# First loads of a routed low-rank kernel split into partition halves over two queues, chunk 0 taken base weights first, seven warm-up products

## The reference

```
base   = x @ W.T                                   # 2048 x 512
logits = x @ Wr.T + 5.0 * one_hot(id of sequence)  # 2048 x 8
topw, topi = top_k(logits, 2); weights = softmax(topw)
gates  = weights at topi, 0 elsewhere              # 2048 x 8
h      = x @ A.T                                   # 2048 x 8 x 16
out    = x + base + 2.0 * sum over experts (h * gates) @ B
```

## Time and profile before

| | |
|---|---|
| median of 3 runs | 80.04 us (79.7, 80.2, 80.04) |
| the profiled execution's own time | 79.61 us |
| its span, first to last instruction | 77.8 us |
| TensorE busy | 74.0 us (95%) |
| VectorE, ScalarE, GpSimd busy | 48.9, 22.4, 22.6 us |

### The profile page before, as it was taken

One profiled execution on the slowest core, in us unless ns is written; L12 is line 12 of the kernel. 1 busy time (PEld: TensorE's weight loads), 2 busy tenths in 40 slices (PEclk: granted clock), 3 DMA queues, 4 the chain that ended last, 5 costly groups with the idle time before them and its releaser, 6 DMA issues.

```text
span 77.8 us, 1631 instructions
## 1 busy us (share of the span) xinstructions
PE 74.0 (95%) x505; PEld 70.3 (90%) x505; DVE 48.9 (63%) x220; ACT 22.4 (29%) x57; POOL 22.6 (29%) x26
## 2 busy tenths in 40 slices
PE   5979999999999999999999999999999999999960
PEld 2349999899999999999999999999999999999950
DVE  0098958879854829283755739283855739787750
ACT  1647901523503314140504113140404023122100
POOL 4039542055160505123060605123060606000000
PEclk9999999999999999999999999999999999999999
DMA  0999991795597399989900000450000072032143
GB/s 10 308 406 401 419 430 60 167 420 230 83 417 313 54 365 440 383 241 402 388 25 0 0 0 0 177 227 0 0 0 0 0 297 107 0 135 95 44 139 135
DMA packets 3893, 14.24 MB, mean 183 GB/s; under 512 B 432, under 2 KB 1328, under 8 KB 3632
## 3 DMA queue, kind: packets, MB, share of 16 engines
q1 hardware_dynamic: 3600, 13.52, 46.8%
q10 hardware_dynamic: 288, 0.67, 2.2%
HBM read 9.99 MB, written 4.19 MB: 182 GB/s over the span
## 4 chain that ended last, share of the span: by engine, by line
PE 90%; DMA 5%; DVE 1%; ACT 1%; SPq 0%; issue 0%
PE heads_ps L429 43%; PE base_ps L429 28%; PE heads_ps L469 5%; PE base_ps L469 5%; DMA first_sb<-in_first 5%; PE base_ps L473 2%; PE heads_ps L473 2%; PE ghT_ps L460 2%; PE base_ps L453 2%; DVE out_sb L421 1%; ACT w_hi L235 1%; SPq L165 0%; PE warm_ps L460 0%
## 5 line engine op out<-in xcount | busy, mean ns | idle before, releaser
L207 POOL TENSOR_TENSOR x_lo<-xT_sb,x_hi 128x512 fp32r<-128x512 f32 x14 | 18.1, 1294 | 39.0 <-ACT x_hi L242 37.2
L429 PE MATMUL heads_ps<-w_hi,x_hi 128*128 128x392 f32 x64 | 22.2, 357 | 0.0
L429 PE MATMUL heads_ps<-w_hi,x_lo 128*128 128x392 f32 x64 | 21.1, 342 | 0.0
L429 PE MATMUL heads_ps<-w_lo,x_hi 128*128 128x392 f32 x64 | 21.1, 340 | 0.0
L429 PE MATMUL base_ps<-w_hi,x_hi 128*128 128x256 f32 x60 | 16.5, 285 | 0.4 <-ACT w_hi L235 0.4
L429 PE MATMUL base_ps<-w_hi,x_lo 128*128 128x256 f32 x60 | 16.7, 281 | 0.0
L429 PE MATMUL base_ps<-w_lo,x_hi 128*128 128x256 f32 x60 | 16.3, 281 | 0.0
L294 DVE TENSOR_TENSOR ghT_lo<-ghT_ps,ghT_hi 128x128 fp32r<-128x128 f32 x15 | 4.3, 290 | 14.9 <-ACT ghT_hi L246 14.8
L246 ACT ACTIVATE ghT_hi<-ghT_ps 128x128 fp32r<-128x128 f32 x15 | 4.1, 275 | 29.5 <-PE ghT_ps L460 29.5
L429 PEld LDWEIGHTS heads_ps<-w_hi,x_hi 128*128 128x128 f32 x64 | 11.7, 188 | 0.9 <-ACT x_hi L232 0.5
L429 PEld LDWEIGHTS base_ps<-w_hi,x_hi 128*128 128x128 f32 x60 | 11.2, 188 | 0.8 <-ACT w_hi L235 0.8
(11 more groups left out here) (51 smaller groups left out, 98.1 us busy)
## 6 DMA issues: line engine op xcount, KB each, us to landing
x_sb<-in_x SPq DMA_DIRECT2D x4, 768.0 KB, 5.6
out<-out_sb SPq DMA_DIRECT2D x4, 768.0 KB, 4.4
xT_sb<-in_xT SPq DMA_DIRECT2D x3, 768.0 KB, 4.3
xT_sb<-in_xT SPq DMA_DIRECT2D x1, 1024.0 KB, 6.3
x_sb<-in_x SPq DMA_DIRECT2D x1, 1024.0 KB, 9.8
first_sb<-in_first SPq DMA_DIRECT2D x2, 454.0 KB, 5.3
out<-out_sb SPq DMA_DIRECT2D x2, 256.0 KB, 2.0
out<-out_sb SPq DMA_DIRECT2D x4, 128.0 KB, 1.7
```

The lines of the kernel that those rows point to most:

```text
L207: nc.gpsimd.tensor_tensor(x_lo[:, s, :], xT_sb[:, t - len(FIRST), :], x_hi[:, s, :].bitcast(FP32), ALU.subtract).then_inc(x_lo_made, 1)
L429: return nc.tensor.matmul(dst, xs[:, s, chunks[k]], ws[:, k, cols], start=(k == 0 and n == 0), stop=(k == KC - 1 and n == last_n))
```

## The change

The loads of `first` are cut by partitions: SyncE loads partitions 0 to 63 and ScalarE partitions 64 to 127 of every piece, by the same function. The pieces are chunk 0's tokens, ids and base weights as one (516 columns), chunk 0's heads weights (392 columns), and chunks 1, 2 and 3 whole. Both halves count up the same semaphore, so every wait on one is now for 32. The base columns come first in the weight table. VectorE rounds the base weights of chunk 0 (its upper part and remainder first), ScalarE the heads weights of chunk 0. TensorE takes chunk 0's three pairs of base products first, then the heads products. The warm-up is seven products instead of nine.

```diff
@@ -25,7 +25,7 @@
 SLOTS = 3
 LANG_BIAS = 5.0
 SCALING = 2.0
-WARM_UP = 9
+WARM_UP = 7
 WIDTH = HEADS + BASE
 
 
...
@@ -141,13 +140,20 @@
         out_made = sem("out_made")
         last_x_placed = sem("last_x_placed")
 
-        heads_cols, base_cols, all_cols = slice(0, HEADS), slice(HEADS, WIDTH), slice(0, WIDTH)
+        base_cols, heads_cols, all_cols = slice(0, BASE), slice(BASE, WIDTH), slice(0, WIDTH)
         chunks = [slice(k * P, (k + 1) * P) for k in range(KC)]
         first_x = [first_sb[:, k, 0:FIRST_X].rearrange("p (t c) -> p t c", c=P) for k in range(KC)]
         ids_at = FIRST_X
         ids_sb = first_sb[:, 0, ids_at:ids_at + 1].bitcast(I32)
         w_sb = first_sb[:, :, FIRST_X + IDS:]
-        w = first[:, :, FIRST_X + IDS:]
+
+        ahead_of = FIRST_X + IDS + BASE
+
+        def load_half(engine, rows):
+            engine.dma_start(first_sb[rows, 0, 0:ahead_of], first[rows, 0, 0:ahead_of]).then_inc(first_landed, 16)
+            engine.dma_start(first_sb[rows, 0, ahead_of:], first[rows, 0, ahead_of:]).then_inc(second_landed, 16)
+            for k in range(1, KC):
+                engine.dma_start(first_sb[rows, k, :], first[rows, k, :]).then_inc(chunk_landed[k - 1], 16)
 
         block = ctx.enter_context(nc.Block())
 
@@ -162,10 +168,7 @@
             def load_xT(t, n, landed):
                 load(xT_sb, xT, t - len(FIRST), n, landed)
 
-            sp.dma_start(first_sb[:, 0, 0:FIRST_X + IDS], first[:, 0, 0:FIRST_X + IDS]).then_inc(x_landed, 16)
-            sp.dma_start(w_sb[:, 0, base_cols], w[:, 0, base_cols]).then_inc(wb_landed, 16)
-            for k in range(2, KC):
-                sp.dma_start(first_sb[:, k, :], first[:, k, :]).then_inc(chunk_landed[k - 1], 16)
+            load_half(sp, slice(0, P // 2))
             load_xT(2, 1, xT_third)
             sp.dma_start(b_sb[:, :], b).then_inc(b_landed, 16)
 
@@ -250,14 +253,13 @@
                 nc.scalar.activation(e2[:, :], top[:, 0:1], ACT.Exp, scale=-1.0,
                                      bias=top[:, 1:2]).then_inc(e2_made, 1)
 
-            act.dma_start(w_sb[:, 0, heads_cols], w[:, 0, heads_cols]).then_inc(wh_landed, 16)
-            act.dma_start(first_sb[:, 1, :], first[:, 1, :]).then_inc(chunk_landed[0], 16)
-            act.wait_ge(x_landed, 16)
+            load_half(act, slice(P // 2, P))
+            act.wait_ge(first_landed, 32)
             chunk_upper(0)
-            act.wait_ge(wb_landed, 16)
-            w_upper(0, base_cols)
+            act.wait_ge(second_landed, 32)
+            w_upper(0, heads_cols)
             for k in range(1, KC):
-                act.wait_ge(chunk_landed[k - 1], 16)
+                act.wait_ge(chunk_landed[k - 1], 32)
                 chunk_upper(k)
                 w_upper(k, base_cols if k == 1 else all_cols)
             x_upper(2, 2, xT_third, 16)
@@ -358,22 +360,22 @@
                 nc.vector.tensor_tensor(w_lo[:, k, cols], w_sb[:, k, cols], w_hi[:, k, cols].bitcast(FP32),
                                         ALU.subtract).then_inc(w_lo_made, 1)
 
-            def heads_upper(k):
-                nc.vector.tensor_copy(w_hi[:, k, heads_cols], w_sb[:, k, heads_cols]).then_inc(wh_hi_made, 1)
-
-            dve.wait_ge(wh_landed, 16)
-            heads_upper(0)
-            dve.wait_ge(wh_hi_made, 1)
-            w_lower(0, heads_cols)
-            dve.wait_ge(w_hi_made, 1)
+            def w_upper(k, cols):
+                nc.vector.tensor_copy(w_hi[:, k, cols], w_sb[:, k, cols]).then_inc(first_hi_made, 1)
+
+            dve.wait_ge(first_landed, 32)
+            w_upper(0, base_cols)
+            dve.wait_ge(first_hi_made, 1)
             w_lower(0, base_cols)
             dve.wait_ge(expert_made, 1)
-            dve.wait_ge(x_landed, 16)
+            dve.wait_ge(first_landed, 32)
             nc.vector.tensor_scalar(bias[:, :], expert[:, :], ids_sb, LANG_BIAS, ALU.is_equal,
                                     ALU.mult).then_inc(bias_made, 1)
-            dve.wait_ge(chunk_landed[0], 16)
-            heads_upper(1)
-            dve.wait_ge(wh_hi_made, 2)
+            dve.wait_ge(w_hi_made, 1)
+            w_lower(0, heads_cols)
+            dve.wait_ge(chunk_landed[0], 32)
+            w_upper(1, heads_cols)
+            dve.wait_ge(first_hi_made, 2)
             w_lower(1, heads_cols)
             dve.wait_ge(w_hi_made, 2)
             w_lower(1, base_cols)
@@ -503,26 +505,27 @@
 
             warm(WARM_UP)
             pe.wait_ge(chunk_hi_made, 1)
-            pe.wait_ge(wh_hi_made, 1)
+            pe.wait_ge(first_hi_made, 1)
+            for t in FIRST:
+                base_product(t, 0, 0)
+            pe.wait_ge(w_lo_made, 1)
+            for t in FIRST:
+                base_product(t, 0, 1)
+            pe.wait_ge(chunk_lo_made, 1)
+            for t in FIRST:
+                base_product(t, 0, 2)
+            pe.wait_ge(w_hi_made, 1)
             for t in FIRST:
                 heads_product(t, 0, 0)
-            pe.wait_ge(w_hi_made, 1)
-            for t in FIRST:
-                base_product(t, 0, 0)
-            pe.wait_ge(chunk_lo_made, 1)
             for t in FIRST:
                 heads_product(t, 0, 2)
-                base_product(t, 0, 2)
-            pe.wait_ge(w_lo_made, 1)
+            pe.wait_ge(w_lo_made, 2)
             for t in FIRST:
                 heads_product(t, 0, 1)
-            pe.wait_ge(w_lo_made, 2)
-            for t in FIRST:
-                base_product(t, 0, 1)
             for k in range(1, KC):
                 pe.wait_ge(chunk_hi_made, k + 1)
                 if k == 1:
-                    pe.wait_ge(wh_hi_made, 2)
+                    pe.wait_ge(first_hi_made, 2)
                 else:
                     pe.wait_ge(w_hi_made, k + 1)
                 for t in FIRST:
@@ -606,7 +609,7 @@
 
     x, W, Wr, A, B = (np.asarray(a) for a in (x, L0_cond_W, L0_cond_Wr, L0_cond_A, L0_cond_B))
     tokens = x.reshape(P, TILES, KC, P)
-    weights = np.concatenate([W[BASE:], A.reshape(ER, D), Wr, W[:BASE]]).reshape(WIDTH, KC, P).transpose(2, 1, 0)
+    weights = np.concatenate([W[:BASE], W[BASE:], A.reshape(ER, D), Wr]).reshape(WIDTH, KC, P).transpose(2, 1, 0)
     xT = tokens.transpose(3, 1, 2, 0)
     ahead = len(FIRST)
     first_x = xT[:, :ahead].transpose(0, 2, 1, 3).reshape(P, KC, FIRST_X)
```

More of the change, by code:

```diff
@@ L94, in cond_resid_program @@
         warm_ps = ps("warm_ps")
-        x_landed = sem("x_landed")
+        first_landed = sem("first_landed")
         xT_third = sem("xT_third")
@@ L102, in cond_resid_program @@
         x_last = sem("x_last")
-        wh_landed = sem("wh_landed")
-        wb_landed = sem("wb_landed")
+        second_landed = sem("second_landed")
         chunk_landed = [sem(f"chunk_landed{k}") for k in range(1, KC)]
@@ L112, in cond_resid_program @@
         bias_made = sem("bias_made")
-        wh_hi_made = sem("wh_hi_made")
+        first_hi_made = sem("first_hi_made")
         w_hi_made = sem("w_hi_made")
```

## The result

The changed kernel takes 82.97 us (median of six executions, 82.63 to 83.43) against 79.89: a ratio of 1.039, 95% interval 1.035 to 1.043. It is **3.1 us slower**; 80.3 was forecast, with a range up to 81.8. The profiled execution is the slowest of the six, 83.43 with a span of 81.6, 3.8 us more than before. An execution over 1.5% above the fastest of its kernel is left out of a ratio; where there are such executions, all times are given.

What follows compares the result with a forecast made beforehand. TensorE's dense stream was taken as the bound, so the end shifts with chunk 1's start: 7.06 against 6.83, +0.23 us. Added to the median of 80.04 this gave 80.27, say 80.3; range 79.5 to 81.8.

Steps and rivals of the forecast that it cites:

- the price of a 64-row issue on ScalarE's queue: Each of three issues added ahead of ScalarE's table load was put at 0.46 us, with bounds 0.34 and 0.68.
- the landing of the halves: First pieces land by about 3.6, covered by 0.76 us until 4.36; chunk 2 must land by 7.75, before at 6.6.
- worth nothing by itself: Before TensorE's first product: seven warm-up products end 0.4 us earlier than nine, but nothing waits for their end; no gain.
- ScalarE's head: At ScalarE's start: five issues push the table load to 3.06 and the first rounding from 3.57 to 4.36, 0.79 us delay.
- The upper bound, 5.02: Latest first rounding on ScalarE, reckoned with 0.68 us for a 64-row issue, the longest load issue.
- First products: TensorE in chunk 0: first base product at 4.83, 0.23 hole for GpSimd's remainders, chunk 1 at 7.06 against 6.83, +0.23 us.
- the half-rate rival: Transfers of half the partitions move at half rate; chunk 3 starts 3.0 us late, 83.0; decides below 304 GB/s; chance 0.22.
- its 10.03 for chunk 2: Moment chunk 2 lands if halves move at 203 GB/s; before, it was taken up at 6.60.
- The milder price that the prediction gave: Halves moving at 270 GB/s add 0.6 us on top of the forecast sum, giving 80.9.
- The clock rival: TensorE's clock falls in the 0.9 us pause before 4.83, products cost double, 1.45 us lost: 81.7; chance 0.10.
- four signs of being wrong: Table load before 2.5; first rounding waits for transfer; ScalarE awaits chunk 2 beyond 7.75; products over 0.18 and 0.12 apart.

Runs made afterwards that it cites:

- ScalarE's issues: Kernel before with three more 64-byte-a-row transfers into an unread spare tile, issued by ScalarE ahead of its table load: 80.15 us, ratio 1.0043.
- the stage by itself: Kernel before with six stages of differently cut transfers put ahead, each waited for; the change's partition halves moved 265 GB/s, 9.69 us a stage.
- the whole-transfer kernel: Changed kernel, seven warm-up products kept, with whole 128-partition transfers on the two queues instead of halves: 81.34 us, ratio 1.017.

## Why the prediction was wrong, step by step

Three steps failed: the price of a 64-row issue on ScalarE's queue, the landing of the halves, and the warm-up that was "worth nothing by itself". None of them gives the 3.1 us alone. Column halves in place of partition halves took back 1.2 (81.79), ten more warm-up products 0.6 (82.39), column halves and twelve warm-up products together 1.9 (81.07). Some 1.2 is left over the kernel before. ScalarE's issues and the column order cost 0.3 each in their own runs; the rest, late landings most likely, no run separates.

- **ScalarE's head: right in mechanism, mis-sized.** The row taken, 0.46, is that of a 128-row issue. The three added issues took 0.64 each, and the first two, which the sum left at the old price, are 64-row issues as well: the third began at 2.24, not 1.66. That makes 0.54 + 0.58 = 1.12, and the first rounding came at 5.48 instead of 4.36. The upper bound, 5.02, failed for the second reason: its 0.68 an issue held for the three, but for all five it would have given about 5.43 (0.75 + 5 x 0.68 + 1.28). Apart from that, 80.27 + 0.66 is 80.9, not the 80.8 of the forecast's own range.
- **First products: right.** TensorE began 0.05 after the rounding, GpSimd's remainders took 0.73 as before. Landing was later than forecast (VectorE at 4.04, not 3.6), but covered.
- **The landing of the halves: put at nothing, and wrong.** Chunk 2 had to land by 7.75, and the sum let it come as before, at 6.6; ScalarE took it up at 9.59. The rate in flight was 265 in the stage by itself and 254 to 301 in the kernel, below the 304 at which the half-rate rival was said to decide. That rival had the right side, and its 10.03 for chunk 2 is near, but its price was too high: TensorE at the low pace asked for chunks 2 and 3 only at 12.19 and 13.95, after their weights were rounded (10.64 and 12.66), and did not wait for them. With seventeen warm-up products chunk 1 takes 2.46 us instead of 1.79, some 0.4 of it behind GpSimd's remainders of the late chunk 1 and 0.25 ahead of chunk 2. The milder price that the prediction gave, 0.6 at 270 GB/s, is near that.
- **The warm-up: put at nothing, and wrong.** In the changed kernel it costs 0.6 us by the medians; in the kernel before, four products cost 1.7, and the change's seven 1.3 to 1.7 in three of four executions. The clock rival had the products at the lower level, with a chance of 0.10; whether they came to it as it says, by a fall in the pause, stays open (below). Its price, 1.45, is that of chunk 3 (1.46 between 7 and 17 products) by luck: it was worked out from 2.9 us at the low pace, while the trace shows 5.7, from 5.95 to about 11.7, part of which the late landings would have cost anyway.
- **The column order: not in the sum at all**, 0.3 us.

Two of the prediction's four signs of being wrong are in the trace: ScalarE waits for chunk 2 beyond 7.75, and products are 0.33 and 0.21 apart.

For the profiled execution, chunk 1 with seventeen warm-up products starts at 8.19, 1.36 late: 0.23 (forecast) and 1.12 (issues). Chunk 3 there is 2.09 late, so 0.73 more comes from late transfers. With seven products it is 3.55 late: 1.46 from the low pace. The remaining 0.25 of 3.80 falls in the tiles behind, where the column order acts. That split is read across two executions, and it depends on the order in which the causes are taken away. That the total lies at the 83.0 of the half-rate rival is a coincidence of terms.

What stays open is when TensorE's clock rises and falls. With seven warm-up products and a pause of 1.07 us the whole-transfer kernel ran at full pace; the kernel before, with the same seven and a pause of 0.40, did not in the traced execution, and one of its other three was as fast as with nine. The seven products take 3.14 to 3.15 us in all these traces, so whether the clock fell in the pause or had not risen by then cannot be told. One trace with nine speaks for the second: where SyncE issues chunk 1, the nine take 4.00 us instead of 3.51, no pause follows, and the first pair of base products still takes 0.43 (5.24 to 5.67), so the clock rose later there than seven products end (3.93). Neither the length of the pause nor the number of products alone decides.

## What to carry to other kernels

Do not cut a transfer by partitions to share it between queues. Leave it whole; if it must be cut, cut by columns (379 GB/s against 265 in the stages here), and check what each further issue pushes back on an engine whose first instruction is awaited. Treat the number of warm-up products as a term with a price of its own: shortening it is not free because nothing waits for its end. A new shape, of a transfer or of its issue, has no row in the old trace, and a bound taken from other shapes has to be put on every instruction of the new shape, not only on those that were added.

## What was not expected of the hardware

A transfer of 64 rows costs more to issue than one of 128 (0.60 against 0.43), and one half alone moved 196 GB/s. The position of a weight block in its row, 0 or 256 columns in, changes a product of 392 columns by about 1% (1.61 against 1.59 us for nine). A small copy on VectorE took 0.57 instead of 0.17 beside a GpSimd operation. And the recorded granted clock read 1.00 in executions whose products plainly ran at half pace, such as the changed kernel's from 6.58 to 8.70; their spacing is the better witness.
